# An S4 convolution beside an int4 SwiGLU block: two phases with operands spilled to DRAM, gate/up in seven block products, down with its whole contraction in PSUM, the convolution in even and odd columns

## The chip, the cores and the metric

One core of one Trainium2 chip. The metric is the device time of one execution in microseconds (us). The engines are TensorE (PE), VectorE (DVE), ScalarE (ACT), GpSimd (POOL) and SyncE (SP, which only issues DMAs here). SBUF is the on-chip memory of 128 partitions, PSUM the eight banks that TensorE accumulates into, DRAM the memory off the engines.

## What is computed

```python
x  = u                                    # 2048 tokens x 1024
xn = layernorm(x)                         # over the 1024
# S4: a kernel K of 1024 taps from 64 states, then a causal convolution along the 1024
K  = irfft-like( c * (k00 - k01 * k10 / (1 + k11)) )      # k..: Cauchy sums over the states
y  = irfft(rfft(xn, 2048) * rfft(K, 2048))[:1024] + D * xn
# int4 SwiGLU, weights as nibbles with a scale and a zero for each 64 inputs
Wg, Wu = dequantize(gate), dequantize(up)                 # 2752 x 1024
Wd     = dequantize(down)                                 # 1024 x 2752
h   = silu(xn @ Wg.T) * (xn @ Wu.T)
out = x + y + h @ Wd.T
```

Both kernels write each f32 operand of a product as a high and a low f16 part (the low one is the residue: the f32 value less its high part), and multiply high x high, high x low and low x high. So each product is three matmuls for every 128 of contraction.

## The kernel before

Tokens are in 4 blocks of 512 (`NB`), the 2752 inner columns in 10 groups of 256 (`NG`, `CH`) and a tail of 192. The transposed `xn` stays in SBUF for the whole kernel as `xh` and `xl`, and the output `acc` (f32, 2048 x 1024) too.

For each group and block, `project` (L616) makes gate and up for two tiles of 128 inner columns with 24 matmuls of 512 columns each, straight: 8 pieces of contraction by 3. ScalarE takes SiLU of gate (L476), VectorE multiplies it with up into `hf` (L867), ScalarE casts the high part `hh` (L485), GpSimd subtracts to get the low part `hl` (L321). `down` (L634) multiplies h with the down weights of the same group in seven products of 2 x 2 blocks, with block sums made by VectorE (`h_sums` L875 to L880, `w_sums` L887 to L892), two halves of 128 tokens each, three matmuls a step. Each of the 14 steps ends with one or two additions from PSUM into `acc` by VectorE (`accumulate`, L904). The second half of `acc` is kept encoded by differences so that seven products need ten additions (GpSimd's `encode`, `decode`, L335 to L346).

The weights of the next group are prepared beside this. Six slabs per group (two each for gate, up and down) come in by SP's `load_slab` (L219, L221). VectorE dequantizes a slab in `w_prep`: two integer operations for the nibbles (L842, L843), a subtraction of the zero (L845), two multiplications by the scale (L848). ScalarE casts (L465) and GpSimd makes the low part (L316).

The order is written out by hand for each engine and held by semaphores. Groups 1 to 8 run in a loop, two per turn. The head (`first_group`) has the layernorm, with statistics on VectorE (L796), normalization on ScalarE (L445), transposes on TensorE (L600), the high part on ScalarE (L451) and the low part on VectorE (L807). The S4 kernel's small chain (`numerators`, `denominators`, `resolvent`, `roots`, `kernel_columns`, `kernel_scale`) runs inside `tail_group`, beside the tail of the SwiGLU. The convolution (L776) is last: for each of 16 token tiles and 2 halves of the output row, matmuls of `xh`, `xl` with a strip of shifted kernels, 512 or 256 columns wide, and one addition into `acc` (L1162), which SP stores.

Of the kernel before, what the change touches and what calls it, by code (L numbers as in the profile page):

```python
# [7 lines left out]
P = 128  # L8
GROUP = 64
CH = 2 * P  # L10
NG = I // CH
TAIL = (I - NG * CH) // 2
TA = P - TAIL
TB = TAIL - TA
SB = 512
NB = S // SB
KC = H // P
NT = S // P
SLAB = 512
L = H  # L20
M8 = L // P

XS_LOG = 10
XS, WS, HS = 2.0 ** XS_LOG, 2.0 ** 12, 2.0 ** -2

# [7 lines left out]

HALF = SB // 2
A11, A12, A22, S2, S3, S4, S1 = range(7)
B11, B21, B22, T3, T2, T1, T4 = range(7)  # L40
# [5 lines left out]
DB = len(STEPS)  # L46
DG = NB * DB
EPS = 1e-5


def s4_plus_int4_swiglu(nc, x_d, raw_gate, raw_up, raw_down, sz_gate, sz_up, sz_down,
                        tail_gate, tail_up, tail_down, tsz_gate, tsz_up, tsz_down,
# [6 lines left out]
    with ctx:  # L59
        def sb(name, shape, dt=f32):  # L60
            return ctx.enter_context(nc.sbuf_tensor(name, shape, dt))

        def sem(name):
            return ctx.enter_context(nc.semaphore(name))


        acc = sb("acc", [P, NT, H])
        xh = sb("xh", [P, KC, S], f16)
        xl = sb("xl", [P, KC, S], f16)
        w_gu = [sb(f"w_gu{i}", [P, 2, 2, KC, CH], f16) for i in range(2)]  # L70
        w_dn = sb("w_dn", [P, 2, 7, SB], f16)
        hh = sb("hh", [P, 2, 7, HALF], f16)
        hl = sb("hl", [P, 2, 7, HALF], f16)
        sil = sb("sil", [P, 2, SB])
        hf = sb("hf", [P, 2, SB])
        raw = sb("raw", [P, 2, SLAB], i32)
        sz = sb("sz", [P, 2, 2 * SLAB])
        wf = sb("wf", [P, 2, 2 * SLAB])
        ident = sb("ident", [P, P])
        stats = sb("stats", [P, 2, 2, 6])  # L80
        mv = sb("mv", [P, NT, 2])
        negm = sb("negm", [P, NT])
        vs = sb("vs", [P, NT])
        rstd = sb("rstd", [P, NT])
        nmr = sb("nmr", [P, NT])
        half = sb("half", [P, 1])
        par = sb("par", [P, 5, 2])
        vcb = sb("vcb", [P, NS, 2])
        bpb = sb("bpb", [P, NS])
        vw = sb("vw", [P, 8])  # L90
        sc = sb("sc", [P, 8])
        d_sb = sb("d_sb", [1, 1])
        cs8 = sb("cs8", [P, 2, M8])
        e = sb("e", [P, 24, M8])
        kcol = sb("kcol", [P, M8])
        zrow = sb("zrow", [1, 2 * P])
        kabs = sb("kabs", [P, M8])
        kmx = sb("kmx", [P, 1])
        ksc = sb("ksc", [P, 2], i32)

        xn = w_gu[1][:, :, :, :, :].rearrange("p a b k c -> p (a b k c)").bitcast(f32)\
            .rearrange("p (j h) -> p j h", j=4)
        s4w = w_gu[1][:, :, :, :, :].rearrange("p a b k c -> p (a b k c)").bitcast(f32)\
            .rearrange("p (j h) -> p j h", j=4)
        strip = w_gu[1][:, 0, :, :, :].rearrange("p b k c -> p b (k c)")\
            .rearrange("p b (n t) -> p b n t", n=2)
        angle = sz
        kshift = wf
        dft = raw[:, 0, 0:2 * P].bitcast(f32).rearrange("p (j a) -> p j a", j=2)
        flip = raw[:, 0, 2 * P:3 * P].bitcast(f32)  # L110
        twiddle = raw[:, 1, 0:P].bitcast(f32)
        krow = raw[0:M8, 1, P:2 * P].bitcast(f32)


        pg = [ctx.enter_context(nc.psum_tensor(f"pg{i}", [P, SB], f32)) for i in range(2)]
        pu = [ctx.enter_context(nc.psum_tensor(f"pu{i}", [P, SB], f32)) for i in range(2)]
        po = [ctx.enter_context(nc.psum_tensor(f"po{i}", [P, SB], f32)) for i in range(4)]

        kpad = nc.dram_tensor("kpad", [CH + L], f32, kind="Internal").ap()


        x_in = [sem(f"x_in{j}") for j in range(4 + NB - 1)]
        slab_in = [sem(f"slab_in{j}") for j in range(2)]
        ident_in, par_in, tab_in, kpad_out, kshift_in, out_done = \
            (sem(n) for n in ("ident_in", "par_in", "tab_in", "kpad_out", "kshift_in", "out_done"))
        stat_done, rstd_done, xn_done, xt_done, xhi_done, xlo_done = \
            (sem(n) for n in ("stat_done", "rstd_done", "xn_done", "xt_done", "xhi_done", "xlo_done"))
        gate_done, up_done, down_done, silu_done, hf_done, hhi_done, hlo_done, acc_done = \
            (sem(n) for n in ("gate_done", "up_done", "down_done", "silu_done", "hf_done", "hhi_done",
                              "hlo_done", "acc_done"))  # L130
        wprep_done, whi_done, wlo_done, dve_order = \
            (sem(n) for n in ("wprep_done", "whi_done", "wlo_done", "dve_order"))
        dve_order_loop = sem("dve_order_loop")
        hsum_done, wsum_done, encoded, decoded = \
            (sem(n) for n in ("hsum_done", "wsum_done", "encoded", "decoded"))
        step_done, cauchy_done, s4_read, dft_done, krow_done, kzero_done, kt_done = \
            (sem(n) for n in ("step_done", "cauchy_done", "s4_read", "dft_done", "krow_done",
                              "kzero_done", "kt_done"))
        resolvent_done, roots_done, kcol_done, flip_done, shi_done, slo_done = \
            (sem(n) for n in ("resolvent_done", "roots_done", "kcol_done", "flip_done", "shi_done", "slo_done"))  # L140
        kabs_done, kscale_done = sem("kabs_done"), sem("kscale_done")
        conv_done, conv_added, pool_order = (sem(n) for n in ("conv_done", "conv_added", "pool_order"))

        def words(k, tail):
            return SLAB // 2 if tail and k in (2, 3) else SLAB

        def sz_view(slot, k, tail):

            w = words(k, tail)
            if k >= 4:
                v = sz[:, slot, 0:2 * w].rearrange("p (z w) -> p z w", z=2)
                return [v[:, z:z + 1, :].broadcast_to((P, 2, w)) for z in range(2)]
            v = sz[:, slot, 0:2 * w].rearrange("p (c z w) -> p c z w", c=2, z=2)
            return [v[:, None, :, z, :].broadcast_to((P, 2, 2, w // 2)) for z in range(2)]

        def wf_view(slot, k, tail, dt=f32):
            w = words(k, tail)
            v = wf[:, slot, 0:2 * w]  # L160
            v = v.bitcast(dt) if dt != f32 else v
            if k >= 4:
                return v.rearrange("p (a w) -> p a w", a=2)
            return v.rearrange("p (a c w) -> p a c w", a=2, c=2)

        def w_source(k, tail):
            if k == 5 and not tail:
                return wf[:, 1, SLAB:2 * SLAB]  # L170
            w = 2 * words(k, tail)
            return wf[:, (0, 1, 0, 1, 0, 1, 1, 0)[k], 0:w].rearrange("p (c w) -> p c w", c=4 if k < 4 else 2)

        def w_dest(parity, k, part, tail):
            if k >= 4 and tail:
                return w_dn[:, part, 2 * (k - 4):2 * (k - 4) + 2, :]
            if k == 4:
                return w_dn[:, part, B11:B21 + 1, :]
            if k == 5:
                return w_dn[:, part, B22, :]  # L180
            if k >= 6:
                return w_dn[:, part, T3 + 2 * (k - 6):T3 + 2 * (k - 6) + 2, :]
            return w_gu[parity][:, k // 2, part, 4 * (k % 2):4 * (k % 2) + 4, 0:words(k, tail) // 2]


        def h_source(i):
            if i == 0:
                return hf[:, 0, 0:HALF]
            return hf[:, i % 2, :].rearrange("p (a s) -> p a s", a=2)

        def h_dest(buf, b, i):
            return buf[:, b % 2, 0, :] if i == 0 else buf[:, b % 2, 2 * i - 1:2 * i + 1, :]

        def tail_h(buf, b, t):

            return buf[:, b % 2, 2 * t:2 * t + 2, :].rearrange("p a s -> p (a s)")

        FIRST = 0
        LOOP = (1, NG - 1)

        block = ctx.enter_context(nc.Block())


        @block.sync
        def _(sp):
# [57 lines left out]
            for k in range(6):  # L263
                load_slab(1, k)
# [983 lines left out]
```

## Time and profile before

| | |
|---|---|
| median of 3 runs | 1552.93 us (1552.26 to 1554.44) |
| span of the profiled execution, first to last instruction | 1550.4 us |
| TensorE busy | 1454.5 us, 94% |
| VectorE busy | 1114.3 us, 72% |
| GpSimd busy | 444.5 us, 29% |
| ScalarE busy | 263.0 us, 17% |
| moved by DMA | 73.28 MB, mean 47 GB/s |

The runs' times are of the whole device execution; the profile gives for its own execution the span alone. "Busy" of TensorE is the union of matmuls whose ends are modelled and which overlap, so a duration of 379 ns of one doesn't mean a distance of 379 ns between two. A VectorE or GpSimd instruction counts as busy from its start to its end, whatever it is held up by inside. The clock of TensorE is given as a share of its full speed.

### The profile page before, as it was taken

The page shows a single profiled execution, that of the slowest core. Times are in us where ns is not written, and L with a number is a line of the kernel's source. Part 1 is how long each engine was busy: PE and PEld are TensorE (multiplying, and loading weights), DVE is VectorE, ACT ScalarE, POOL GpSimd, SP SyncE. Part 2 cuts the span into 40 slices and gives each one's busy share as a digit, 9 for nine tenths or more (in the row PEclk, how much of TensorE's full clock was granted, in tenths as well). Part 3 has the DMA queues.
Part 4 walks back from the last instruction along what each step waited for, and adds up shares of the span by engine and source line. Part 5 has one row for each costly group of instructions (what it writes and reads, how often), then busy time and mean ns, then how long its engine had stood idle before and what let it go on. Part 6 is the DMA issues. An engine that isn't in the chain of part 4 may idle for free.

```text
span 1550.4 us, 18942 instructions
## 1 busy us (share of the span) xinstructions
PE 1454.5 (94%) x6701; PEld 664.0 (43%) x6701; DVE 1114.3 (72%) x1674; ACT 263.0 (17%) x400; POOL 444.5 (29%) x311
## 2 busy tenths in 40 slices
PE   5698989999999999999999999999999996789999
PEld 3354434444444444444444444444444442333454
DVE  5677968778768877867887786877877868744322
ACT  3343111112112102111211111111211210111000
POOL 2263433223214313413333232222322415300000
PEclk8799999999999999999999999999999998889999
DMA  7311111101100110110110110110110011100122
GB/s 229 114 42 41 42 40 52 51 21 38 65 23 21 61 42 21 52 52 19 43 57 14 53 49 14 53 50 21 41 62 21 19 40 32 47 1 28 55 82 82
DMA packets 25369, 73.28 MB, mean 47 GB/s; under 512 B 2994, under 2 KB 3899, under 8 KB 25019
## 3 DMA queue, kind: packets, MB, share of 16 engines
q1 hardware_dynamic: 25131, 71.95, 13.9%
q8 instruction: 60, 0.98, 0.3%
q14 instruction: 34, 0.28, 0.1%
q10 hardware_dynamic: 144, 0.07, 0.0%
HBM read 63.62 MB, written 8.39 MB: 46 GB/s over the span
## 4 chain that ended last, share of the span: by engine, by line
issue 47%; PE 25%; POOL 14%; DVE 8%; DMA 4%; ACT 2%; SPq 0%; POOLq 0%; DVEq 0%; ACTq 0%
PE po L776 7%; POOL hl L321 7%; PE pu L616 5%; POOL w_gu L316 4%; PE po L634 4%; PE pg L616 4%; PE po L648 2%; DMA sz<-in_tsz_down 2%; DVE acc L904 2%; POOL w_dn L316 2%; PE pg L663 1%; DMA sz<-in_sz_up 1%; DMA sz<-in_sz_gate 1%; PE pu L663 1%; DVE wf L845 1%
## 5 line engine op out<-in xcount | busy, mean ns | idle before, releaser
L904 DVE SCALAR_TENSOR_TENSOR acc<-po,acc 128x512 f32<-128x512 f32 x800 | 492.2, 680 | 55.5 <-PE po L634 55.5
L321 POOL TENSOR_TENSOR hl<-hf,hh 128x512 f16<-128x512 f32 (+1 forms) x160 | 199.2, 1255 | 784.9 <-ACT hh L485 784.9
L616 PE MATMUL pu<-xh,w_gu 128*128 128x512 f16 x1280 | 398.4, 383 | 13.8 <-POOL w_gu L316 13.8
L616 PE MATMUL pg<-xh,w_gu 128*128 128x512 f16 x1280 | 398.7, 383 | 11.7 <-issue 8.1
L634 PE MATMUL po<-w_dn,hh 128*128 128x512 f16 x1120 | 336.1, 382 | 39.6 <-DVE acc L904 39.2
L616 PE MATMUL pg<-xl,w_gu 128*128 128x512 f16 x640 | 245.4, 383 | 0.0
L616 PE MATMUL pu<-xl,w_gu 128*128 128x512 f16 x640 | 244.9, 383 | 0.0
L634 PE MATMUL po<-w_dn,hl 128*128 128x512 f16 x560 | 213.6, 381 | 0.0
L485 ACT ACTIVATE hh<-hf 128x512 f16<-128x512 f32 (+1 forms) x160 | 87.9, 572 | 716.8 <-DVE hf L867 514.8
L616 PEld LDWEIGHTS pg<-xh,w_gu 128*128 128x128 f16 x1280 | 126.5, 99 | 168.2 <-issue 16.1
L616 PEld LDWEIGHTS pu<-xh,w_gu 128*128 128x128 f16 x1280 | 126.2, 99 | 167.9 <-POOL w_gu L316 14.8
L634 PEld LDWEIGHTS po<-w_dn,hh 128*128 128x128 f16 x1120 | 107.4, 98 | 180.6 <-DVE acc L904 41.9
L867 DVE SCALAR_TENSOR_TENSOR hf<-pu,sil 128x512 f32<-128x512 f32 x80 | 55.0, 688 | 172.2 <-PE pu L616 152.1
L848 DVE SCALAR_TENSOR_TENSOR wf<-wf,sz 128x512 f32<-128x512 f32 (+1 forms) x128 | 136.3, 1105 | 2.2
L316 POOL TENSOR_TENSOR w_gu<-wf,w_gu 128x1024 f16<-128x1024 f32 (+1 forms) x44 | 101.6, 2308 | 57.7 <-ACT w_gu L465 57.7
L845 DVE TENSOR_TENSOR wf<-wf,sz 128x1024 f32<-128x1024 int32 (+1 forms) x64 | 100.0, 1562 | 2.2
L776 PE MATMUL po<-w_gu,xh 128*128 128x512 f16 (+1 forms) x384 | 97.2, 344 | 0.0
L476 ACT ACTIVATE sil<-pg 128x512 f32<-128x512 f32 x88 | 52.0, 591 | 261.0 <-PE pg L616 208.3
L616 PEld LDWEIGHTS pg<-xl,w_gu 128*128 128x128 f16 x640 | 63.2, 99 | 76.4 <-issue 3.2
L616 PEld LDWEIGHTS pu<-xl,w_gu 128*128 128x128 f16 x640 | 63.1, 99 | 76.2 <-issue 2.2
L316 POOL TENSOR_TENSOR w_dn<-wf,w_dn 128x1024 f16<-128x1024 f32 (+1 forms) x42 | 81.5, 1961 | 30.9 <-ACT w_dn L465 30.9
L634 PEld LDWEIGHTS po<-w_dn,hl 128*128 128x128 f16 x560 | 55.1, 98 | 67.1 <-issue 1.8
(152 smaller groups left out, 926.3 us busy)
## 6 DMA issues: line engine op xcount, KB each, us to landing
sz<-in_sz_gate SPq DMA_DIRECT2D x20, 512.0 KB
sz<-in_sz_up SPq DMA_DIRECT2D x20, 512.0 KB
sz<-in_sz_down SPq DMA_DIRECT2D x20, 512.0 KB
out<-acc SPq DMA_DIRECT2D x15, 512.0 KB, 2.6
acc<-in_x SPq DMA_DIRECT2D x3, 2048.0 KB, 25.4
raw<-in_raw_gate SPq DMA_DIRECT2D x20, 256.0 KB
raw<-in_raw_up SPq DMA_DIRECT2D x20, 256.0 KB
raw<-in_raw_down SPq DMA_DIRECT2D x20, 256.0 KB
```

The lines of the kernel that those rows point to most:

```text
L316: pool.tensor_tensor(w_dest(parity, k, 1, tail), w_source(k, tail), w_dest(parity, k, 0, tail), ALU.subtract).then_inc(wlo_done, 1)
L321: pool.tensor_tensor(h_dest(hl, b, i), h_source(i), h_dest(hh, b, i), ALU.subtract)\
L476: act.activation(out, gate, ACT.Silu, scale=1.0 / (XS * WS)).then_inc(silu_done, 1)
L485: act.activation(h_dest(hh, b, i), h_source(i), ACT.Copy).then_inc(hhi_done, 1)
L616: last = pe.matmul(bank[:, :], w[:, mat, wp, k, t * P:(t + 1) * P], xp[:, k, toks], start=(k == 0 and wp == 0 and xp is xh), stop=(k == KC ...
L634: last = pe.matmul(po[(DB * b + n) % 4][:, :], hp[:, b % 2, ha, i * P:(i + 1) * P], w_dn[:, wp, wb, :], start=(hp is hh and wp == 0), stop ...
L648: last = pe.matmul(po[d % 4][:, :], tail_h(hp, b, t)[0:n, st * P:(st + 1) * P], w_dn[0:n, wp, 2 * t + hd, :], start=(i == 0), stop=(i == l ...
L776: last = pe.matmul(po[d % 4][:, t0 - c * SB:SB], xp[:, k, st * P:(st + 1) * P], strip[:, sp_, nib, t0 - h0:(c + 1) * SB - h0], start=(k == ...
L845: dve.tensor_tensor(w, q, zero, ALU.subtract).then_inc(dve_order_loop, 1)
L848: last = dve.scalar_tensor_tensor(out=w[:, nib], in0=w[:, nib], scalar=WS, in1=scale[:, nib], op0=ALU.mult, op1=ALU.mult)
L867: dve.scalar_tensor_tensor(out=hf[:, t, :], in0=pu[t][:, :], scalar=HS / (XS * WS), in1=sil[:, t, :], op0=ALU.mult, op1=ALU.mult).then_inc ...
L904: last = dve.scalar_tensor_tensor(out=part, in0=po[(DB * b + n) % 4][:, :], scalar=sign / (WS * HS), in1=part, op0=ALU.mult, op1=ALU.add)
```

## The change

The whole kernel is rewritten in two phases.

Phase one computes h. `xn` is kept as the left operands of a 2 x 2 block product: for each half p of the tokens (1024), seven blocks of 512 x 512 (four of them sums of blocks, made by GpSimd in `x_sums`), each as high and low part (`xo`). Against them stands, for each tile t of 128 inner columns, the block [gate, up] in its seven right operands (`wo`, two tiles deep; the sums by VectorE's `t_sum`). One unit is a tile and a half: seven products of 12 matmuls give gate and up for 128 columns and 1024 tokens. The products accumulate in three PSUM banks; ScalarE copies a bank out between two products (`snap_s1`, `snap_u2`, `snap_s5`, `snap_u3`) and VectorE and GpSimd add the copies (`c11`, `c12`, `c22`). There are 42 such units, 4 in a group g, and two tail units of 48 straight matmuls. h goes, again as seven left operands of blocks, in high and low part through a buffer `hs` to DRAM (`h_d`), the seven down operands through two buffers `ds` to DRAM (`w_d`), and the parts of `xn` that the convolution needs to DRAM (`xc_d`). All low parts but those of `xn` are made by GpSimd (`w_low`, `d_low`, `h_low`). The head has eight pairs of token tiles with seven blocks of four transposes each. The S4 kernel's chain is cut into steps that VectorE does in units 5 to 24 (`s4_work`).

Phase two reads the down operands back (`wd`, seven blocks of 2.88 MB, once) and h (`hr`, 0.72 MB for each product and each two of four token tiles). Each of 4 passes x 7 products x 2 runs over the whole contraction of 11 x 128 in PSUM with 33 matmuls, and VectorE adds one bank per product to `acc`, which is loaded with x again and holds one pass. The convolution stands between the products. It is split in even and odd columns of the sequence: three pieces per token tile instead of four, of even, odd, and their sum, each as matmuls of 512, 384, 256 and 128 columns.

The core of the diff:

```diff
-PRODUCTS = ((A11, B11, ((1, 0, 0), (1, 1, 0))), (A12, B21, ((1, 0, 0),)), (S4, B22, ((1, 0, 1),)),
-            (S2, T2, ((1, 1, 0),)), (S3, T3, ((1, 1, 0), (-1, 0, 1))), (S1, T1, ((1, 1, 1),)),
-            (A22, T4, ((1, 1, 0), (-1, 1, 1))))
-STEPS = [(i,) + prod for prod in PRODUCTS for i in range(2)]
+A11, A12, S2, S1, S3, S4, A22 = range(7)
+B11, B21, T2, T1, T3, B22, T4 = range(7)
+BANK = (0, 1, 0, 2, 0, 2, 0)
+OPENS = (True, True, False, True, False, False, False)
...
+            def load_slab(m, words, scales):
+                slot = m % 2
+                if m >= 2:
+                    sp.wait_ge(deq_done, m - 1)
+                sp.dma_start(raw[:, slot, :], words).then_inc(slab_in[slot], 16)
...
+            # SP, third unit of group g
+                    store_h(g, 1, A11)
+                    load_up(2 * g + 2)
+                    store_w(g - 1, T1)
+                    store_w(g - 1, T3)
+                    store_h(g, 1, S3)
+                    load_gate(2 * g + 3)
...
+            # SP, between the phases
+            for i in range(2):
+                sp.wait_ge(ds_out[i], 16 * ((77 + 1 - i) // 2))
+            load_wd(0)
+            sp.wait_ge(prod_done, products_before(42))
+            load_wd(1)
+            sp.wait_ge(prod_done, products_before(43))
+            load_hr(0, 0, 0)
+            load_hr(0, 0, 1)
...
+            # ACT, third unit of group g
+                    d_high(g - 1, T1)
+                    snap_s1(n + 2)
+                    d_high(g - 1, T3)
+                    h_high(g, 1, S3)
+                    snap_u2(n + 2)
+                    d_high(g - 1, T2)
+                    d_high(g - 1, T4)
+                    snap_s5(n + 2)
...
+            def d_high(g, j):
+                q = 7 * g + W_POS[j]
+                if j in T_POS:
+                    act.wait_ge(dsum_done, 4 * g + T_POS[j] + 1)
...
+                if q >= 2:
+                    act.wait_ge(ds_out[q % 2], 16 * (q // 2))
+                act.activation(ds[:, q % 2, 0, :], d_place_of(j), ACT.Copy).then_inc(dhi_done, 1)
...
+            def products(n, t, p, j):
...
+                if p == 0:
+                    pe.wait_ge(wlo_done, 7 * t + W_POS[j] + 1)
+                if j == 0 and n >= 2:
+                    pe.wait_ge(sil_done, 2 * (n - 2) + 2)
...
+                if j in (2, 4, 5, 6):
+                    pe.wait_ge(snap_done, 4 * n + {2: 1, 4: 2, 5: 3, 6: 4}[j])
+                bank = banks[BANK[j]][n % 2]
+                for k in range(KH):
+                    for wp, xp in ((0, 0), (0, 1), (1, 0)):
+                        done = pe.matmul(bank[:, :], wo[t % 2][:, j, wp, k * P:(k + 1) * P], xo[p][:, j, xp, k, :],
...
+            def down(sp_, j, s):
...
+                for k in range(KC):
+                    for hp, wp in ((0, 0), (0, 1), (1, 0)):
+                        done = pe.matmul(bank[:, :], hr[slot][:, k, hp, :], wd[j][:, k, wp, :],
...
+            def conv(c):
...
+                for c4 in range(KH):
+                    for up, wp in ((0, 0), (0, 1), (1, 0)):
...
+                        done = pe.matmul(bank[:, c4 * P:SB], u, strip[kind][:, wp, 0:SB - c4 * P],
...
+            def dequantize(m, w):
+                slot = m % 2
+                dve.wait_ge(slab_in[slot], slab_arrived(m))
+                q, r = w.bitcast(i32), raw[:, slot, :]
+                dve.tensor_scalar(q[:, 0, :], r, 4, 15, ALU.arith_shift_right, ALU.bitwise_and)
+                link(dve.tensor_scalar(q[:, 1, :], r, 15, None, ALU.bitwise_and))
+                link(dve.tensor_tensor(w, q, sz[:, slot, 1:2, :].broadcast_to((P, 2, 512)), ALU.subtract))
+                dve.scalar_tensor_tensor(out=w, in0=w, scalar=WS, in1=sz[:, slot, 0:1, :].broadcast_to((P, 2, 512)),
+                                         op0=ALU.mult, op1=ALU.mult).then_inc(deq_done, 1)
```

(The three comment lines on SP and ACT are added here to say where the lines stand.)

## Rows read from the trace of the kernel before

**Rows 1.** The page: engine, busy us, share of the span, instructions.
```profile
PE 1454.5 (94%) x6701; PEld 664.0 (43%) x6701; DVE 1114.3 (72%) x1674; ACT 263.0 (17%) x400; POOL 444.5 (29%) x311
```
**Rows 2.** Windows: stretch, its us, busy (count) by engine, clock, DMA share, GB/s.
```profile
540.00:660.00 120.00, 118.89 (x551) 53.57 (x550) 94.90 (x139) 20.48 (x32) 37.14 (x24) 1.00 0.12 40
...
1260.00:1320.00 60.00, 46.65 (x209) 20.61 (x208) 45.35 (x69) 5.87 (x11) 26.63 (x15) 0.89 0.16 47
...
1440.00:1500.00 60.00, 60.00 (x327) 31.63 (x326) 14.94 (x21) 0.00 (x0) 0.00 (x0) 1.00 0.18 71
```
**Rows 3.** TensorE's waits: us in total, times, longest.
```profile
PE po L634 <- DVE acc L904: 39.2, 14, 13.3
```
**Rows 4.** The chain of waits: start, us, what.
```profile
54.07 5.23 PE pu L616 x12
...
135.46 5.18 PE pg L616 x24
```
**Rows 5.** Timeline, 737 to 757 us, of GpSimd, then VectorE: start, us, instruction.
```profile
737.29 1.16 POOL L321 TENSOR_TENSOR hl<-hf,hh 128x512 f16<-128x512 f32 x1 [12.44 <-ACT hh L485]
743.20 3.50 POOL L321 TENSOR_TENSOR hl<-hf,hh 128x512 f16<-128x512 f32 x2 [4.75 <-ACT hh L485]
746.67 2.57 POOL L316 TENSOR_TENSOR w_gu<-wf,w_gu 128x1024 f16<-128x1024 f32 x1
...
743.63 2.06 DVE L845 TENSOR_TENSOR wf<-wf,sz 128x1024 f32<-128x1024 int32 x1
745.73 4.06 DVE L848 SCALAR_TENSOR_TENSOR wf<-wf,sz 128x512 f32<-128x512 f32 x2
...
754.72 1.23 DVE L845 TENSOR_TENSOR wf<-wf,sz 128x1024 f32<-128x1024 int32 x1
755.98 1.29 DVE L848 SCALAR_TENSOR_TENSOR wf<-wf,sz 128x512 f32<-128x512 f32 x2
```
**Rows 6.** Timeline, 1303 to 1309 us, of GpSimd, then VectorE.
```profile
1303.78 2.33 POOL L343 TENSOR_TENSOR acc<-acc 128x1024 f32<-128x1024 f32 x1
1306.19 2.34 POOL L346 TENSOR_TENSOR acc<-acc 128x1024 f32<-128x1024 f32 x1
...
1303.94 2.19 DVE L951 COPY vw<-e 64x8 f32<-64x8 f32 x1
1306.15 0.17 DVE L952 TENSOR_SCALAR vw<-e 64x4 f32<-64x4 f32 x1
1306.22 2.33 DVE L953 COPY vw<-e 64x4 f32<-64x4 f32 x1
```
**Rows 7.** Groups by form: count, busy us, mean ns, idle before them.
```profile
L904 DVE SCALAR_TENSOR_TENSOR acc<-po,acc 128x512 f32<-128x512 f32 x800 | 492.2, 680 | 55.5 <-PE po L634 55.5
L321 POOL TENSOR_TENSOR hl<-hf,hh 128x512 f16<-128x512 f32 x120 | 172.3, 1449 | 685.2 <-ACT hh L485 685.2
...
L842 DVE TENSOR_SCALAR wf<-raw 128x512 int32<-128x512 int32 x62 | 30.0, 484 | 20.3 <-DMA sz<-in_sz_up 17.9 <-DMA sz<-in_sz_gate 2.3
...
L485 ACT ACTIVATE hh<-hf 128x512 f16<-128x512 f32 x120 | 71.3, 624 | 547.5 <-DVE hf L867 354.0 <-DVE hf L878 192.8 <-DVE hf L880 0.7
...
L807 DVE TENSOR_TENSOR xl<-po,xh 128x512 f16<-128x512 f32 x32 | 20.1, 683 | 13.6 <-ACT xh L451 13.5
```
**Rows 8.** Timeline of TensorE in the head.
```profile
8.94 5.75 PE L600 MATMUL po<-ident,w_gu 128*128 128x128 f32 x24 [8.94 <-ACT w_gu L445]
```
**Rows 9.** Windows of 5 us in the head; the last two numbers are DMA share, GB/s.
```profile
25.00:30.00 5.00, 5.00 (x17) 1.96 (x16) 1.13 (x2) 1.06 (x1) 2.12 (x1) 0.66 1.01 221
30.00:35.00 5.00, 5.00 (x25) 2.29 (x24) 2.36 (x4) 0.00 (x0) 0.00 (x0) 1.00 1.02 352
```
**Rows 10.** SP's issue of a slab, and a store's size and us to landing.
```profile
438.96 0.57 SPq L221 DMA_DIRECT2D sz<-in_sz_gate  x1
...
out<-acc SPq DMA_DIRECT2D x15, 512.0 KB, 2.6
```

More of the change, by code:

```diff
@@ new lines, in slab_down, with slab_tail, slab_arrived, down_slab @@
+def slab_down(g, half):
+    if g == 10:
+        raise ValueError("the last rows have slabs of their own")
+    if half == 0:
+        return 6 if g == 0 else 7 + 6 * (g - 1) + 4
+    return 7 + 6 * g + 1
+def slab_tail(kh, half):
+    return 63 + 2 * kh + (1 - half)
+def slab_arrived(m):
+    n = 32 * (m // 2 + 1)
+    return n + 32 if m >= 63 else n
+def down_slab(g, kh, half):
+    return slab_tail(kh, half) if g == 10 else slab_down(g, half)
+def s4_plus_int4_swiglu(nc, x_d, raw_gate, raw_up, raw_v, raw_down, raw_tail,
+                        sz_gate, sz_up, sz_v, sz_down, sz_tail,
@@ L141, in s4_plus_int4_swiglu @@
[L141 to L172, printed above, removed]
@@ L300, in _ @@
+            store_out(3, 0)
+            store_out(3, 1)
+            for s in range(2):
+                sp.wait_ge(out_done[s], 128)
         @block.gpsimd
@@ L436, in _ @@
+            for p in range(2):
+                for j in L_ORDER:
+                    h_low(NG, p, j)
         @block.scalar
@@ L909, in tail_accumulate @@
[L909 to L915 removed]
+                    link(dve.tensor_scalar(q, r, 15, None, ALU.bitwise_and))
@@ L1158, in _ @@
[L1158 to L1163 removed]
+                link(dve.tensor_scalar(ksc[:, 0:2], ksc[:, 0:2], 23, None, ALU.logical_shift_left))
@@ new lines, in _ @@
+            x_stats(0)
+            x_stats(1)
+            gate(0)
+            for j in range(7):
+                x_low(0, j)
+            x_stats(2)
+            up(0)
+            t_sum(0, T1)
+            t_sum(0, T3)
+            for j in range(7):
+                x_low(1, j)
+            x_stats(3)
+            t_sum(0, T2)
+            t_sum(0, T4)
+            for j in range(7):
+                x_low(2, j)
+            x_stats(4)
+            for j in range(7):
+                x_low(3, j)
@@ new lines, in _ @@
+            gate(1)
+            for j in range(2):
+                x_low(4, j)
+            x_stats(5)
+            c11(0)
+            for j in range(2, 6):
+                x_low(4, j)
+            up(1)
+            x_low(4, 6)
+            t_sum(1, T1)
+            t_sum(1, T3)
+            for j in range(2):
+                x_low(5, j)
+            c12(0)
+            t_sum(1, T2)
+            h_first(0, 0, 0)
+            t_sum(1, T4)
+            x_stats(6)
+            for j in range(2, 4):
+                x_low(5, j)
@@ new lines, in _ @@
+            h_second(0, 0, 0)
+            for j in range(4, 7):
+                x_low(5, j)
+            x_stats(7)
+            for j in range(2):
+                x_low(6, j)
+            c11(1)
+            for j in range(2, 7):
+                x_low(6, j)
+            for j in range(2):
+                x_low(7, j)
+            c12(1)
+            h_first(1, 1, 0)
+            for j in range(2, 7):
+                x_low(7, j)
+            h_second(1, 1, 0)
+            h_s3(0, 0)
+            gate(2)
```

2204 lines of the change are left out of this document (1346 added, 858 removed).

## The prediction

> **What bounds the kernel now.** The page's busy shares come first [rows 1]: TensorE 94%, VectorE 72%, GpSimd 29%. Then the windows [rows 2]: between 540 and 660 us TensorE is busy 118.89 of 120 us at clock 1.00, while the stretch 1260 to 1320 has holes and a clock of 0.89. The largest of TensorE's waits [rows 3] is small, 39.2 us for VectorE's accumulation. The chain of waits [rows 4] gives the pitch: 24 matmuls of 512 columns in 5.18 us, 0.2158 us each (2.4 GHz); after an idle spell 12 take 5.23 us, about twice that (1.2 GHz). The kernel issues 3840 + 288 matmuls for gate/up, 1680 + 160 for down, and 576 in the convolution worth 480 full ones (384 of 512 and 192 of 256 columns): 6448 full matmuls, times 0.2158 = 1391.5 us of the 1550.4. So it is bound by matmul columns, with some 159 us of head, seams and tail.
>
> **Where the second limit lies.** GpSimd and VectorE get in each other's way. In rows 5 GpSimd's instruction at 737.29 and VectorE's two at 754.72 and 755.98 stand alone: 1.16, 1.23 and 1.29 us. At 743.20 two such of GpSimd take 3.50 us, and VectorE's next to them 2.06 and 4.06 [rows 5]. It comes out exactly if one holds the memory at a time: 1.1 + 1.1 + 2.13 for GpSimd, 1.2 + 0.55 + 0.55 for VectorE, 6.6 us in all, and 743.20 to 749.79 is 6.6. It shows at its plainest in copies of 4 and 8 elements, L951 and L953: 2.19 and 2.33 us, each as long as the GpSimd instruction beside it [rows 6]. Operations that read PSUM and one SBUF tile are free of it: the mean of 800 L904 is 680 ns, unchanged beside GpSimd [rows 7].
>
> **TensorE's work after.** Gate/up: 42 units of 7 products of 12 matmuls, 3528, and 2 tail units of 48: 3624 (before 4128, -504). Down: 4 x 7 x 2 x 33 = 1848 (before 1840, +8). Convolution: 48 pieces, each 3 matmuls of 512, 384, 256 and 128 columns, worth 360 (before 480, -120). Together 5832, 616 fewer, 133 us. Transposes rise from 128 to 224 blocks of 128 columns; 24 take 5.75 us, 0.24 each [rows 8], so +23 us.
>
> **The new load beside it.** One group of four units (two tiles, 336 matmuls, 72.5 us of TensorE). GpSimd: 14 weight, 7 down and 14 h residues and 4 additions, 39 instructions of 512 columns. VectorE: 6 slabs (two shifts, one subtraction, one multiply), 12 weight sums, 8 multiplies to h, 8 h sums, all SBUF to SBUF, and 8 PSUM additions. Holding times, from the exact fit above: GpSimd 39 x 1.1 = 43; a slab of VectorE 0.3 + 0.3 (L842 less its start-up [rows 7]) + 1.15 + 1.15 = 2.9, six 17; 28 others x 0.54 = 15; the PSUM additions (8 x 0.68) hold nothing. That is 75 us of one shared resource against 72.5 of TensorE. Before, a group of 119 us of TensorE had about 53 of it (GpSimd 31: 12 h residues of 512 and 4 of 256 columns, 7.5 weight residues of 2.13; VectorE 22: 6 slabs and 20 sums, 16 of them of 256 columns). The lower bound of a group is TensorE's 72.5 + 1.5 = 74; the upper is no overlap at all: VectorE 43 of plain durations plus GpSimd 39 x 1.16 = 45, and a little for in-order waits, 90 to 95. I take 82, the shared 75 at 91% occupancy, because every residue waits for ScalarE's cast, every cast for a sum, and each engine runs in order.
>
> In order, something else is late there too. In the third unit of a group ScalarE casts the down sums between the copies out of PSUM that TensorE's products wait for. The cast of T2 waits for the store of T1, which stands on SP's queue behind a slab load, which waits for VectorE's slab two before. From the end of the second unit: SiLU 0.6, h 0.7, cast 0.6 and residue 1.1, sum 0.6, slab 3.3 to 5, issues 1.3 [rows 10], landing about 2.6 [rows 10], casts 1.2, some 12 to 14 us; the copy is due at 4 x 2.59 = 10.4 to 13. A stall of 0 to 4 us per group, within the step from 74 to 82. ScalarE itself has 59 operations of 0.62 [rows 7] = 37 us per group, hidden as a load.
>
> **Stage by stage, in profile time.**
> Head, to the start of unit 4: 165 us. VectorE must take three pairs of token tiles through statistics (4 x 0.64 + small = 3.3 each, five of them), two slabs (3.3 each), sums and 22 low parts at 0.62 (L807) before the first product; with ScalarE's casts in order in between, about 57 us. Then units 0 and 1 carry 14 products and 112 transposes: 36 + 28 on TensorE, with waits 69, to 126. Units 2 and 3: 39. Bounds 145 and 185.
> Nine groups at 82: 738. The small chain of the S4 kernel moves from the tail into groups 1 to 6, some 140 small operations which each may queue behind a GpSimd instruction [rows 6]: 0 to 38 us, I take 20. What hides it is slack on VectorE, and at 82 us a group there is little. Units 40 and 41: 40. Now at 963.
> Seam: the two tail units are 20.7 us. Beside them the last down rows are dequantized (two slabs wait for the two before), then seven products go through two staging buffers, each pair at about 4.5 us of cast, residue, issue and landing: stored 27.5 us after unit 41. Only then does SP issue the first weight block, 2.88 MB; the second and the first two h blocks (0.72 MB each) are queued with it, 7.2 MB. The nearest rows show 221 and 352 GB/s at full DMA share [rows 9]; I take 300: 24 us + 2.5. Phase two starts 54 us after unit 41, at 1017, TensorE idle 33 us (with 352: 50 us; with 221: 63).
> Phase two: 1848 x 0.2158 = 399; the convolution 144 x (0.216 + 0.162 + 0.11 + 0.10) = 85, where the 128-wide ones are taken at the 0.10 of their weight load rather than 0.054, since the 256-wide keep the full-rate pitch (327 in 60 us [rows 2]). On its first pass TensorE uses a block of 14 to 17 us while the queue brings 8.5, 6.7, 6.4 and 4.3 MB per block: 28 - 14, 22 - 17.5, 21 - 17.5, nothing: 23 us of stall (16 at 352, 51 at 221). After that a block needs 1.5 MB in 17.5 us, hidden. VectorE has 14 + 20 accumulations and 20 sums per pass of 121 us, hidden, and GpSimd is idle. 507 us, to 1524. A cold start 3 and the last addition and 1 MB stores 5: 1532.
> Around it: the page's execution has a span of 1550.4 and the median of the runs is 1552.93; I add the same 2.5: 1535 us.
> Edits at nothing: the reading of x twice and the spill stores (5.3 MB per group, with the slabs 10 MB in 82 us, 120 GB/s against 221 or more); if that cover went, the staging buffers would come free late and ScalarE stall. Accumulation in PSUM leaves 56 of the 800 + 32 additions to acc and none of GpSimd's encodings; TensorE had hidden them but for its 39.2 us of waits [rows 3], so this itself gives only VectorE's time for the new sums.
>
> The Trainium skill (DMA: Bandwidth & Descriptors, section Bandwidth) has 341 GB/s for a load of 1 MB and more for larger ones. The window of 352 GB/s agrees, that of 221 doesn't; by the Trainium skill the seam and the first pass would be about 10 us shorter, 1525.
> The Trainium skill (TensorE: Matmul & The Clock Gate, Back-to-back issue gap) gives a sustained 131 ns for a matmul of 512 columns and 81 for 128. This trace has 215.8 ns for the first, so that rate doesn't hold here; by the 81 ns of the Trainium skill the convolution would be 3 us shorter.
>
> **Rivals.**
> A, TensorE stays the limit: the shared port is only nearly full, two units of slack cover the waits. For it: the loop before reached 98%. Against: the load of 75 is above 72.5. 165 + 9 x 74 + 0 + 37 + 54 + 507 + 8 = 1437, so 1440 us.
> B, slower: the port, fully serial. In phase one GpSimd's instructions and VectorE's SBUF ones never overlap, and idle times of in-order waits come on top: 90 us a group, the S4 work 38, units 40 and 41 44: 165 + 810 + 38 + 44 + 54 + 507 + 8 = 1626, so 1629 us. It decides from 84 us a group on, where the total passes 1553. For it: the copies that wait for all of a GpSimd instruction [rows 6]. Against: the overheads in VectorE's plain durations (0.16 us each) do overlap.
> C, slower: the spill comes back at 221 GB/s or less: the seam +9, the first pass +28, the mixed stores +3: 1575 us. For it: the window at 25 us, with share 1.01. Against: 352 five us later.
>
> **Chances.** Forecast 0.45 (own range 1490 to 1585), A 0.28, B 0.15, C 0.12. Two thirds of the forecast's own range lies below 1550, with A that is 0.58 faster by over 0.2% (3 us, about what a measurement of this kernel can tell); within 0.2% 0.04; slower 0.38. The range over the cases, leaving the far halves of A and B: 1430 to 1625.
>
> **What would show it.** A group's period of 82 (74: A, 90: B); GpSimd's 512-column residues at a mean well above 1.45 us and busy over 65% in phase one; VectorE's L848-like multiply at 2 us; TensorE waiting for GpSimd's wo. The seam: a hole of 33 us with the clock down, ended by a DMA. Phase two at 0.99 busy and 118 us per pass. It is wrong if the group is near 74, if the head ends far from 165, or if the first pass waits for wd by more than 60 us.

## The result, and the profile after

| | before | after |
|---|---|---|
| median of the runs (us) | 1553.68 (1552.26 to 1559.24) | 1841.95 (1840.34 to 1845.39) |
| ratio, 95% interval | | 1.1853, 1.1822 to 1.1885 |
| span of the profiled execution (us) | 1550.4 | 1838.5 |
| mean granted clock | | 0.89 |

The change makes the kernel slower by 18.5%. The forecast was 1535 us, with a range up to 1625: it missed the size, and for the likeliest case the sign.

The page of the kernel after, busy time by engine (against [rows 1]):

```profile
PE 1416.8 (77%) x6297; PEld 647.0 (35%) x6297; DVE 938.3 (51%) x1162; ACT 423.3 (23%) x738; POOL 630.7 (34%) x483
```

No engine is full. The windows (stretch, its us, busy and count by engine, clock, DMA share, GB/s; the answer to [rows 2]) say which phase it is:

```profile
600.00:720.00 120.00, 91.91 (x374) 38.66 (x373) 73.92 (x102) 36.47 (x65) 58.85 (x44) 0.86 0.28 88
...
1504.00:1622.00 118.00, 118.00 (x602) 57.24 (x600) 39.61 (x57) 3.77 (x6) 0.00 (x0) 1.00 0.44 140
```

The second window is one pass of phase two, with TensorE busy in all of its 118 us, as forecast. In phase one TensorE has holes and a granted clock of 0.86, while VectorE is busy 62% and GpSimd 49%: neither is the limit. By stages of the profiled time, from the starts of the units:

| stage | forecast | measured |
|---|---|---|
| head, to the first copy of unit 4 (some 3 us behind its start) | 168 | 208.0 |
| from there to the first copy of unit 41 (9 x 82 + 20 + 20) | 778 | 1041.4 |
| from there to the end of unit 41 | 17 | 15.2 |
| seam: end of unit 41 to phase two (TensorE idle) | 54 (33) | 56.9 (36.0) |
| phase two, cold start and last stores | 515 | 517 |

Two stages are wrong, the head by 40 us and the units by 263. The view of waits over the whole kernel (who waited for whom: us in total, times, longest) points at the cause of the large one:

```profile
ACT ds L798 <- DMA w_d<-ds: 386.7, 33, 16.8
POOL ds L608 <- ACT ds L798: 377.1, 36, 13.9
DVE hf L1381 <- POOL u L623: 271.8, 31, 17.1
...
PE px L1108 <- ACT s L819: 143.8, 28, 9.2
...
PE pz L1108 <- ACT s L831: 131.8, 23, 11.0
```

Read it upward from TensorE: it waits for ScalarE's copies out of PSUM (L819, L831), 276 us in all. ScalarE is busy 23%, so it must be waiting itself, and it is: 386.7 us for the store of a down operand out of `ds`. The DMA part of the page gives size and us from issue to landing:

```profile
h_d<-hs SPq DMA_DIRECT2D x154, 256.0 KB, 2.4
...
w_d<-ds SPq DMA_DIRECT2D x77, 256.0 KB, 8.8
```

Two stores of one size: that of h lands in 2.4 us, that of the down operands in 8.8. The timeline of the third unit of one group, ScalarE and then SP's queue (start, us, instruction, idle time before it), shows why:

```profile
606.63 0.61 ACT L798 ACTIVATE ds<-wf 128x512 f16<-128x512 f32 x1
...
607.62 0.62 ACT L798 ACTIVATE ds<-wf 128x512 f16<-128x512 f32 x1
...
624.71 1.26 ACT L798 ACTIVATE ds<-wf 128x512 f16<-128x512 f32 x2 [11.77 <-DMA w_d<-ds]
625.88 0.58 ACT L831 ACTIVATE s<-pz 128x512 f32<-128x512 f32 x1
...
642.52 1.25 ACT L798 ACTIVATE ds<-wf 128x512 f16<-128x512 f32 x2 [14.03 <-DMA w_d<-ds]
...
693.64 0.63 ACT L798 ACTIVATE ds<-wf 128x512 f16<-128x512 f32 x1 [13.64 <-DMA w_d<-ds]
```

```profile
614.75 0.35 SPq L307 DMA_DIRECT2D raw<-in_raw_up  x1
615.14 0.55 SPq L308 DMA_DIRECT2D sz<-in_sz_up  x1
615.73 0.95 SPq L347 DMA_DIRECT2D w_d<-ds  x2
```

Both `ds` buffers are cast by 608.2 (T1 and T3). Their stores are issued at 615.73 only, since SP first waits for VectorE to free a slab buffer, and they land at 624.7, nine us later, behind the scales of that slab (L308). ScalarE's next instruction is the cast into the first buffer (T2); behind it in its order stands the copy at 625.88 that TensorE needs. The same comes again at 642.52: B11 and B21 of the next down rows wait for the stores of T2 and T4, issued at 633.90 behind the next slab. And it comes once more at 693.64, in the first unit of the next group: B22 waits for the store of B11, which was cast at 642.5 but is issued at 681.85 only, since it stands behind the stores of h and three slabs.

Why nine us? The scales are loaded as 4 rows, each repeated over 32 partitions. A window of the kernel before, 2 us behind the issue of such a load [rows 10], shows what it uses:

```profile
441.00:446.00 5.00, 5.00 (x25) 2.24 (x24) 3.06 (x6) 0.42 (x1) 0.67 (x1) 1.00 0.26 96
```

DMA share 0.26 and 96 GB/s: a quarter of the 16 engines, for some 5 us. A store issued behind it that is spread over all engines then has a part of its data behind that backlog; e1_spread below tests it. The Trainium skill (DMA: Bandwidth & Descriptors, Why a DMA increments its semaphore by 16 and not by 1) says that a DMA runs on the largest number of engines up to 16 that divides the slowest dimension of both sides; with 4 rows against 128 partitions that is 4 of 16, and the share of 0.26 agrees.

### The profile page after: what moved, and what is told of

Its sections match the earlier page's. It is cut to its first block and busy times, and to the rows that moved or that the text cites. A ratio compares the mean times of both kernels' runs of the same rounds, so it can differ in the third digit from the quotient of the medians.

```text
span 1838.5 us, 16992 instructions
## 1 busy us (share of the span) xinstructions
PE 1416.8 (77%) x6297; PEld 647.0 (35%) x6297; DVE 938.3 (51%) x1162; ACT 423.3 (23%) x738; POOL 630.7 (34%) x483
## 5 line engine op out<-in xcount | busy, mean ns | idle before, releaser
L1108 PE MATMUL px<-xo,wo 128*128 128x512 f16 x2016 | 515.6, 414 | 146.6 <-ACT s L819 143.8
L1108 PE MATMUL pz<-xo,wo 128*128 128x512 f16 x1008 | 268.5, 423 | 131.9 <-ACT s L831 131.8
L1108 PEld LDWEIGHTS px<-xo,wo 128*128 128x128 f16 x2016 | 209.6, 105 | 430.9 <-ACT s L819 125.3
L1193 PE MATMUL px<-wd,hr 128*128 128x512 f16 x1056 | 235.2, 382 | 36.0 <-DMA hr<-h_d 36.0
L618 POOL TENSOR_TENSOR hs<-hf,hs 128x512 f16<-128x512 f32 x154 | 213.5, 1398 | 133.1 <-ACT hs L812 126.1
L599 POOL TENSOR_TENSOR wo<-wf,wo 128x512 f16<-128x512 f32 x147 | 212.5, 1462 | 109.5 <-ACT wo L779 109.5
L1108 PEld LDWEIGHTS pz<-xo,wo 128*128 128x128 f16 x1008 | 106.0, 107 | 284.8 <-issue 187.3
L1193 PEld LDWEIGHTS px<-wd,hr 128*128 128x128 f16 x1056 | 102.8, 98 | 157.3 <-issue 41.0
L798 ACT ACTIVATE ds<-wf 128x512 f16<-128x512 f32 x77 | 47.9, 625 | 407.4 <-DMA w_d<-ds 386.7
L1193 PE MATMUL pz<-wd,hr 128*128 128x512 f16 x528 | 116.6, 379 | 0.0
L1108 PE MATMUL py<-xo,wo 128*128 128x512 f16 x504 | 115.6, 379 | 0.0
```

What stands on the lines that cost most here:

```text
L599: pool.tensor_tensor(w_dest(t, j, 1), w_place_of(j), w_dest(t, j, 0), ALU.subtract).then_inc(wlo_done, 1)
L618: pool.tensor_tensor(hs[:, j, :, 1, :], h_place_of(p, j), hs[:, j, :, 0, :], ALU.subtract)\
L1108: done = pe.matmul(bank[:, :], wo[t % 2][:, j, wp, k * P:(k + 1) * P], xo[p][:, j, xp, k, :], start=(OPENS[j] and k == 0 and wp == 0 and x ...
L1193: done = pe.matmul(bank[:, :], hr[slot][:, k, hp, :], wd[j][:, k, wp, :], start=(OPENS[j] and k == 0 and hp == 0 and wp == 0), stop=(k == ...
```

## Experiments

All times are medians; each ratio is to the runs of the kernel before on the same chip (medians 1552.2 to 1553.7 us), with its 95% interval. Runs e1 to e4 are from one chip, e5 to e7 and b1 from a second, e8 to e11 from a third; across these, compare the ratios. The last column is from the first copy of unit 4 to that of unit 41, in the profiled execution.

| kernel | us | ratio | units 4 to 41 |
|---|---|---|---|
| after | 1841.95 | 1.185 (1.182 to 1.189) | 1041.4 |
| e1_spread | 1716.10 | 1.105 (1.103 to 1.107) | 921.3 |
| e2_order | 1595.18 | 1.028 (1.026 to 1.029) | 796.6 |
| e3_both | 1564.37 | 1.007 (1.005 to 1.008) | 775.1 |
| e4_nospill | 1573.35 | 1.013 (1.011 to 1.015) | 771.5 |
| e5_snap | 1558.81 | 1.004 (1.002 to 1.006) | 762.3 |
| e6_seam | 1546.73 | 0.996 (0.995 to 0.997) | 761.4 |
| e7_half | 1466.53 | 0.945 (0.943 to 0.947) | 677.0 |
| e8_seam2 | 1513.61 | 0.974 (0.971 to 0.977) | 761.0 |
| e9_c22 | 1486.47 | 0.958 (0.954 to 0.961) | 736.8 |
| e10_res | 1495.26 | 0.963 (0.960 to 0.965) | 742.8 |
| e11_dummy | 1531.72 | 0.987 (0.983 to 0.991) | 740.2 |
| b1_spread (from before) | 1538.43 | 0.990 (0.987 to 0.993) | |

**The scales on all engines.**

```diff
-                sp.dma_start(sz[:, slot, :, :]..., scales[:, None, :].broadcast_to((4, 32, 1024)))
+                for q in range(4):
+                    sp.dma_start(sz[32 * q:32 * q + 32, slot, :, :]..., scales[q:q + 1, :].broadcast_to((32, 1024)))
```

> Changed: each slab's scales and zeros come by four DMAs of 32 partitions instead of one whose outer dimension is 4. Theory (ScalarE, in order, sits before the cast of a down operand until the store two before has landed, and that store is slow because the one scales DMA of the slab queued ahead of it runs on a quarter of the DMA engines, share 0.25 at 90 GB/s for 5 us): the stores of ds land in about 3.5 us instead of 8.8, each of the three waits of a group shortens by 5 us, the group goes from 108 to about 94 us, the whole to about 1705 us. Rival (the memory port that GpSimd and VectorE share sets the group): the group stays within 3 us of 108 and the whole above 1800.

The page and the waits of e1_spread:

```profile
w_d<-ds SPq DMA_DIRECT2D x77, 256.0 KB, 3.7
```

```profile
ACT ds L800 <- DMA w_d<-ds: 259.3, 33, 17.0
```

126 us less, from the form of one small load. The store lands in 3.7 us, yet ScalarE still waits 259 us: that is the late issue, behind the slab loads. Landing is as expected, the whole 11 us above the expected 1705.

**The order of SP's queue.**

```diff
                     store_h(g, 1, A11)
-                    load_up(2 * g + 2)
                     store_w(g - 1, T1)
                     store_w(g - 1, T3)
+                    load_up(2 * g + 2)
                     store_h(g, 1, S3)
-                    load_gate(2 * g + 3)
                     store_w(g - 1, T2)
                     store_w(g - 1, T4)
+                    load_gate(2 * g + 3)
```

and the stores of B11 and B21 at the head of the next group.

> Changed: on SP's queue the stores of the down operands stand ahead of the slab loads that they stood behind; everything else as after. Theory: T1 and T3 are issued 5 us sooner and land in 2.5 us instead of 9, T2 and T4 the same, B11 and B21 long before they are waited for; ScalarE's waits for these stores (387 us in all) fall under 60, the group goes from 108 to about 80 us, the whole to about 1580 us. If only the slow scales DMA counted and not the order, it would be no better than the run that spreads it (1705). Rival (shared port): above 1800.

```profile
ACT ds L799 <- DMA w_d<-ds: 72.1, 16, 8.9
```

247 us less, with not one operation changed. The miss: 72 us of waits are left where under 60 were expected, and the whole is 15 us above the expected 1580. Both edits together:

> Both edits at once. Theory: the waits are gone by the order alone, so the groups are those of the order run (80 us) and only the head gains, 5 to 10 us, since its slabs land sooner: about 1570 us. If each had its own share of the wait, the sum of the two gains. Rival (shared port): above 1800.

278 us less. They overlap (126 + 247 = 373), because a store ahead of the slab is ahead of its scales too. The whole came out as expected, but not for the reason given: the head gains nothing over e2_order (unit 4 at 205 against 203 us), the units lose another 21 us. They now take 775 us, 778 were forecast.

**No spill of the down operands.** The base is the kernel after, with its order and its scales in four rows; phase two reads the stored rows of the last group eleven times.

```diff
             def store_w(g, j):
+                if g < 10:
+                    return
...
-                if q >= 2:
-                    act.wait_ge(ds_out[q % 2], 16 * (q // 2))
+                if 2 <= q:
+                    act.wait_ge(dlo_done, q - 1)
...
```

> Left out: the down operands of groups 0 to 9 are cast and their low parts made, but not stored; ScalarE's cast waits for GpSimd's low part two before instead of the store; phase two reads the last group's rows eleven times, the same bytes. Theory: no DMA is left in that loop, the group is what the shared port and the in-order engines leave, 78 to 82 us, the whole 1560 to 1600. Rival (the shared port sets the 108): the group stays near 108, since GpSimd and VectorE have all their instructions.

```profile
w_d<-ds SPq DMA_DIRECT2D x7, 256.0 KB, 2.0
```

Nothing is gained over e3_both: the three last groups have the same 78.6 us in both, unit by unit. So in these groups no wait for this store is left in e3_both's pace, and neither the spill's volume nor the form of the scales costs them anything.

**ScalarE's copies first.**

```diff
                 silu_second(n - 1)
-                h_high(g - 1, 1, A12)
                 snap_s1(n)
+                h_high(g - 1, 1, A12)
...
                 snap_u2(n)
-                h_high(g - 1, 1, S4)
                 snap_s5(n)
+                h_high(g - 1, 1, S4)
```

the same in the other units, and `s4_work` behind `h_first`.

> e3_both with ScalarE's copies of the banks (snap_s1, snap_s5) put ahead of the casts of h that wait for VectorE, and the S4 work of each unit put behind the sum that frees a bank. If what is left of the longer groups is ScalarE's order alone: the group's long unit (24.2 us in e3_both) falls to about 19 us, the late groups go 78.6 to about 74 us, the stretch with S4 work loses 10 to 15 us, total about 1530 us. If the lock between GpSimd and VectorE sets the pace, the wait only moves to the next bank: groups stay at 77 to 79 us, total over 1552 us.

Missed: 5.6 us instead of 34, and even that is at the edge of what can be told (the two intervals touch). The long unit of 24.2 us went, but others of 19 to 21 came, and the late groups stay at 78 to 80 us. The wait moved, as that run's rival had it. That the lock between GpSimd and VectorE made it move is not shown: TensorE's largest wait is now 24.4 us for the copy `u` (L840), and e9_c22 below takes the late groups to 75 us by moving one sum out of GpSimd's queue.

**What GpSimd's residues cost.** e7_half halves them, shown at those of h:

```diff
-                pool.tensor_tensor(hs[:, j, :, 1, :], h_place_of(p, j), hs[:, j, :, 0, :], ALU.subtract)
+                c = 4 if g + p == 0 else 2
+                pool.tensor_tensor(hs[:, j, 0:c, 1, :], h_place_of(p, j)[:, 0:c, :], hs[:, j, 0:c, 0, :], ALU.subtract)
```

> e5_snap with the low parts of the down operands, of h and of gate/up computed for half of their columns only (the other half of each low part keeps old data), so that GpSimd's instructions are half as long and hold the port half as long. If the port still costs in e5_snap: VectorE's busy time falls by over 80 us, the stretch with S4 work and the late groups shorten, total 15 to 30 us below e5_snap. If ScalarE's order was all, within 5 us of e5_snap.

Busy time by engine, page of e5_snap, then of e7_half:

```profile
PE 1350.5 (87%) x6297; PEld 633.8 (41%) x6297; DVE 954.3 (61%) x1162; ACT 425.5 (27%) x738; POOL 644.7 (41%) x483
```

```profile
PE 1323.0 (91%) x6297; PEld 630.1 (43%) x6297; DVE 800.9 (55%) x1162; ACT 422.4 (29%) x738; POOL 451.7 (31%) x483
```

92 us less, three times the upper end expected. VectorE does the same work in 153 us less. Its shifts show the stretching best (groups by form, e5_snap and e7_half; count, busy us, mean ns):

```profile
L1281 DVE TENSOR_SCALAR wf<-raw 128x512 int32<-128x512 int32 x63 | 51.3, 814 | 0.0
```

```profile
L1285 DVE TENSOR_SCALAR wf<-raw 128x512 int32<-128x512 int32 x63 | 30.7, 487 | 0.0
```

In e7_half all but a few units take 18.1 to 18.3 us, TensorE's own 84 x 0.2158. Is it the port that is held, or the later low part? e11_dummy puts time back behind each halved residue, in an instruction whose result nobody uses:

```diff
+                    pool.tensor_tensor(idle[0][:, :, :], ident[:, None, :].broadcast_to((P, 2, P)),
+                                       ident[:, None, :].broadcast_to((P, 2, P)), ALU.subtract).then_inc(idle_done, 1)
```

> e7_half with, behind each halved low part, a second GpSimd instruction of the same length on a constant, for which nothing waits. GpSimd is then as long busy as in e5_snap, but each low part is ready earlier. If it is the time that GpSimd holds the port and its queue, the gain of e7_half (92 us) goes: total 1540 to 1560 us. If it was how late a single low part comes, the total stays under 1485 us.

```profile
PE 1334.7 (87%) x6297; PEld 630.4 (41%) x6297; DVE 880.2 (58%) x1162; ACT 426.5 (28%) x738; POOL 754.1 (49%) x838
```

```profile
DVE hf L1415 <- POOL u L655: 136.9, 30, 7.8
```

In between, so neither half of the expectation held: 65 of the 92 us come back, VectorE's busy time rises by 79 again. It is no clean split. GpSimd is busy 754 us against 645 in e5_snap, so more time was put back than had been taken. And the added instructions do stand in somebody's way: VectorE waits 137 us for the sum `u` that GpSimd makes behind them (46 in e7_half, 97 in e5_snap). So GpSimd's time costs this kernel, through VectorE's stretched instructions and through GpSimd's own queue; how much is each, and how much is that a low part comes earlier, is not shown. The Trainium skill (SBUF — State Buffer, SBUF: two separate sides) calls the port pair that the two engines share an exclusive lock for the whole instruction, when VectorE's reads two SBUF inputs or runs in a 2-port mode; the shifts' 814 against 487 ns fit that, if they run in such a mode, which no view shows.

**The seam.** e6_seam gives the first two operands of phase two the places that unit 42 frees, loads them ahead of stores that they stood behind, and moves the last casts and sums to match:

```diff
-        w_place = [W0, W0 + 22 * K1, X0, X0 + 22 * K1, ...
+        w_place = [X0, X0 + 22 * K1, W0, W0 + 22 * K1, ...
...
+            store_w(NG, B11)
             sp.wait_ge(prod_done, products_before(43))
...
+            load_wd(0)
             load_hr(0, 0, 0)
             load_hr(0, 0, 1)
...
+            store_w(NG, B21)
```

> e5_snap with the seam changed: operands 0 and 1 of phase two get the places in xo[0], which unit 42 frees, and are loaded with their h ahead of the last stores; the tail's scales come by DMAs of 32 partitions; kshift is loaded at the end of the last unit. If the seam's idle time of TensorE (35.8 us in e3_both) is the late issue behind the last stores and 5.8 MB queued ahead, it falls to 5 to 15 us and the waits for kshift and strip (25 us) halve: total 30 to 40 us below e5_snap, about 1495 us. If it is bandwidth, the idle time stays above 25 us and the total within 12 us of e5_snap.

TensorE, then VectorE, of e6_seam:

```profile
1006.29 9.33 PE L1217 MATMUL px<-wd,hr 128*128 128x512 f16 x33 [7.29 <-issue]
...
1080.66 3.38 PE L1244 MATMUL pv<-strip,xc 128*128 128x512 f16 x12 [40.41 <-DVE strip L1762]
```

```profile
1075.67 0.69 DVE L1748 SCALAR_TENSOR_TENSOR acc<-px,acc 128x512 f32<-128x512 f32 x1 [44.51 <-DMA acc<-in_x]
```

The hole fell from 35.8 us in e3_both (38.2 in e5_snap) to 7.3 us, and 40.4 came 70 us later: 12 gained of the 30 expected. e8_seam2 moves that one too: strips ahead of the last casts of h, `acc` loaded as soon as its place is free.

```diff
+            sp.wait_ge(hf_done, 88)
+            load_acc(0, 0)
+            load_acc(0, 1)
             for i in range(2):
                 sp.wait_ge(ds_out[i], 16 * ((77 + 1 - i) // 2))
             load_wd(2)
```

> e6_seam with the strips of the convolution cast ahead of the last five casts of h for the second rows, and the loads of x into acc issued as soon as their place is free. e6_seam's idle time before the first product fell to 7.3 us, but TensorE then waited 40.4 us for the strips, behind VectorE's wait of 44.5 us for acc. If that is order alone: this wait falls below 8 us, total 1546.7 - 35 = about 1512 us. If DMA bandwidth of the seam is the limit (29 MB from 995 to 1080 us at up to 400 GB/s), the wait comes back as one for wd or hr and the total stays over 1535 us.

As expected. TensorE's waits from 960 to 1200 us are five, of 7.1 us at most and 22.7 in all. The seam was order, not bandwidth.

**GpSimd relieved without leaving anything out.**

```diff
             def h_second(n, t, p):
+                dve.wait_ge(snap_done, 4 * n + 4)
+                dve.tensor_tensor(u3[:, :], u3[:, :], s5[:, :], ALU.add).then_inc(u2_done, 1)
                 dve.wait_ge(sil_done, 2 * n + 2)
```

> e8_seam2 with the sum u3 + s5 of each unit on VectorE instead of GpSimd. VectorE's waits for that sum (87 us in units 5 to 41 of e6_seam) go, VectorE gets 42 x 0.68 = 29 us more, GpSimd 42 x 1.2 = 50 us less. If GpSimd's queue (the sum stands behind low parts) sets the pace: groups 79 to about 75 us, total 15 to 25 us below e8_seam2, about 1493 us. If VectorE's own time is the bound: no gain, or up to 10 us more.

27 us less for moving 42 additions. VectorE had waited 83 us for them in e8_seam2, since on GpSimd each stood behind low parts; the last three groups take 75 to 76 us, 76 to 81 before. The window over the units of e9_c22 shows what is next:

```profile
205.00:900.00 695.00, 646.42 (x2942) 289.10 (x2941) 652.48 (x709) 285.48 (x511) 452.57 (x305) 0.98 0.44 131
```

VectorE is busy 94%, TensorE 93%. Four residues a group more on VectorE gain nothing:

```diff
+            def t_low(t):
+                for j in (T2, T4):
+                    dve.wait_ge(wlo_done, 7 * t + W_POS[j])
+                    dve.wait_ge(whi_done, 7 * t + W_POS[j] + 1)
+                    dve.tensor_tensor(w_dest(t, j, 1), w_place_of(j), w_dest(t, j, 0), ALU.subtract).then_inc(wlo_done, 1)
```

> e9_c22 with the low parts of T2 and T4 of the projections (4 per group) on VectorE instead of GpSimd from t = 3 on. If the sum of both engines' times on the shared port is the bound (1.15 us on GpSimd against 0.68 us on VectorE): 4 x 0.47 = 1.9 us less per group, 15 to 20 us less in all. If VectorE's own order is the bound: each waits about 1 us for ScalarE's cast in VectorE's queue, 36 x 1.7 us, the total rises by 10 to 40 us.

8.8 us slower than e9_c22: GpSimd has 60 us less (556.7 against 616.2), VectorE's busy time stays (1012.1 against 1013.0) though it does 36 instructions more, so it is stretched less. The rival of that run expected 10 to 40 us from waits for ScalarE's casts in VectorE's queue; the trace has no such wait among VectorE's largest (the largest is 11 us for SiLU, 5 in e9_c22). Of the 10.6 us between the two spans 5 come before unit 4 and 6 in the units; what makes them is not shown.

**The same load in the kernel before**, with e1_spread's edit.

> The kernel before with its scales loaded by four DMAs of 32 partitions in place of one with four rows. If the slow scales DMA costs the kernel before only at its start (VectorE's 17.9 us of waits for sz_up): 1553 to about 1540 us. If each load is hidden already: no change. If it costs in every step of the loop as in the kernel after: below 1520 us.

```profile
L843 DVE TENSOR_SCALAR wf<-raw 128x512 int32<-128x512 int32 (+1 forms) x64 | 32.5, 508 | 1.3 <-DMA sz<-in_sz_up 1.2
```

14 us of 1553: the head's wait of 17.9 us for `sz` [rows 7] is 1.2 now. In its loop each such load was hidden (the middle half of its gate/up matmuls takes 615 us in the kernel before and 616 here); the kernel after put a store behind it.

## Why the prediction was wrong

**The failed step** is the one on the third unit: "The cast of T2 waits for the store of T1, which stands on SP's queue behind a slab load [...] A stall of 0 to 4 us per group". The mechanism is the one that occurred. Its size was not: the landing was taken as "about 2.6" from a store of `out` with nothing slow ahead of it [rows 10], and measured 8.8. And it was counted once a group, where it comes three times: T2 and T4 behind T1 and T3, B11 and B21 behind T2 and T4, B22 behind B11. The two others stood in the forecast at nothing, and so did the spill stores, by a mean of 120 GB/s against 221 or more; a mean says nothing of what stands just ahead of a store. Measured: ScalarE waits 11.77 + 14.03 + 13.64 us for these three, in a group whose period was 110 us, not 82. Without it (e3_both) the units take 775 us for the forecast's 778, and 266 of the 269 us between the two spans are there.

**The missed row.** The share 0.26 stood in the trace of before, right behind a slab's issue [rows 10]. In that kernel nobody waits behind that load once the head is over.

**The head**, 165 against 205: the first product came 8 us late, and units 0 and 1 took 101 us instead of 69. TensorE waits 43.4 us of the head for VectorE's low parts, 31 of them in these two units. No run changed the order there, so the cause stays open.

**The port.** The shared load of 75 us against TensorE's 72.5 in a group, with 82 as the value taken, came out near in number: e3_both has 78.6 in the late groups. But the agreement of 775 with 778 is in part luck: the first six groups, with the S4 work, take 78 to 93 us, 43 more than six late ones where 20 were forecast, and this makes up for most of the 3.4 us that each group is below 82. Of the signs named, GpSimd's share in phase one holds (510.8 of 775 us, 66%); its residues' mean (1.37 to 1.44 us for "well above 1.45") and VectorE's multiply (1.43 us for 2) don't, and TensorE waits for ScalarE's copies, not for GpSimd's `wo`. e7_half shows that GpSimd's time is a real cost. Rival A's 74 is nearly reached by e9_c22, 75 to 76 in late groups with nothing left out; so a part of the step from 74 to 78.6 was the place of one sum in GpSimd's queue. Rival B's 90 is only passed beside the S4 work.

**Seam and phase two** agree in their sums, 56.9 for 54 and 517 for 515, and this is luck: the terms don't. In the seam the first load of a down operand is issued 38.9 us after unit 41 (27.5 forecast), and what it needs lands 18 us later (26.5 forecast), at a rate above the 300 GB/s taken:

```profile
1304.00:1321.50 17.50, 0.00 (x0) 0.02 (x1) 3.32 (x5) 1.70 (x3) 3.52 (x3) 0.50 0.97 394
```

That refutes rival C's rate of 221. By the Trainium skill's 341 GB/s (DMA: Bandwidth & Descriptors, Bandwidth) 7.2 MB would take an estimated 21 us; of the two figures it is the nearer one to this trace. In phase two the forecast had 23 us of waits for the down operands. TensorE never waits for them; it waits for two things that stood at nothing, the shifted kernels and the strips made of them, and the convolution is cheaper than its 85 us:

```profile
PE pv L1234 <- DMA kshift<-kpad: 13.2, 1, 13.2
PE pv L1220 <- DVE strip L1736: 12.6, 1, 12.6
...
1394.86 1.79 PE L1220 MATMUL pv<-strip,us 128*128 128x512 f16 x12
1396.49 7.29 PE L1193 MATMUL px<-wd,hr 128*128 128x512 f16 x33
```

A piece of 12 matmuls takes 1.63 us from start to start, 78 us for the 48; by columns alone (1280 x 3 at 512 in 0.2158 us) it is 1.62. So the 128-wide matmul kept the full rate, about 0.054 us, and not the 0.10 of its weight load.

**Where the gain of 616 matmuls (133 us) went**: the forecast had already set 115 us against it (the head, groups of 82 us for 72.5 of TensorE, the S4 work, the seam, the first pass), which left 18; then 266 us of stall and 40 of head came on top. With the scales spread, both orders mended, the sum moved and the seam overlapped it appears: e9_c22 takes 1486 us, ratio 0.958, below the kernel before and below b1_spread's 1538.

## What to carry to other kernels

When an engine in order both frees a bank for TensorE and refills a staging buffer, price the refill as the whole chain (what the store's issue waits for, what lies ahead of it on the same DMA engines, landing), and count every place where it stands; put the copies and the stores ahead of what may wait. Look at the DMA share right behind each small load before something is queued behind it: a share near 0.25 where nothing else moves says a quarter of the engines. Check a forecast term by term, also where its sum came out. After a stall is mended expect the next wait on the same engine, as in e5_snap and e6_seam.

## What the runs showed of the hardware

- A load of 512 KB with 4 rows repeated over 32 partitions ran at share 0.26 and 96 GB/s, and stores of 256 KB behind it landed in 8.8 us; as four loads of 32 partitions, in 3.7; ahead of it, in 2.6 to 2.8.
- Halving GpSimd's residues took 153 us off VectorE's busy time for the same 1162 instructions; 355 GpSimd instructions on a constant gave 79 of it back.
- Moving 36 residues from GpSimd to VectorE left VectorE's busy time as it was (1013.0, then 1012.1 us).
- Matmuls of 512, 384, 256 and 128 columns, three of each, took 1.63 us, in proportion to their columns.
- Reading spilled operands back ran at 394 GB/s over 17.5 us, at a DMA share of 0.97.
